# Attention products for TensorE written in its own reading order, with turned copies of v and of the weighted values

## The chip, the cores and the metric

The kernel runs on one core of one Trainium2 chip. The metric is the device time of one execution in microseconds (us); the median of three runs counts. The engines are PE (TensorE), DVE (VectorE), ACT (ScalarE), POOL (GpSimd) and SP (SyncE, which issues DMAs).

## The reference, cut to what matters

Seven convolutions turn 64 clips into 64 x 12 tokens of 192 channels; then come one attention layer and one layer of experts. The attention is a Nystrom attention: every sequence of 12 tokens is padded in front to 64, so that each of the 64 landmarks is one token, 52 of them zero.

```python
qkv = x @ w_qkv.T                       # 12 heads of 16 channels
sim = einsum('bhid,bhjd->bhij', q * scale, k)
attn1 = attn2 = attn3 = softmax(sim)    # one token per landmark
z = attn2.T / (max(col) * max(row))
for _ in range(6):
    xz = attn2 @ z
    z = 0.25 * z @ (13 * I - xz @ (15 * I - xz @ (7 * I - xz)))
out = attn1 @ (z @ (attn3 @ v))
out = out @ w_proj.T + b_proj
```

## The kernel before, in words

Attention is done lane by lane: each of the 128 partitions holds one sequence and half of the heads (HL = 6). The 52 padded tokens are folded into one, so each head has a matrix of R = 13 by 13 (`smat`), and v has SEQ = 12 rows of DH = 16. A matrix product per lane is not a thing TensorE can do, so every small product is made of two steps: all elementwise products of one output row (for example 6 heads x 13 columns x 13 terms = 1014 elements), then a sum over the terms.

The class `RowSums` (L771) describes one such job. It divides the output rows among the engines:

- `sum_pe`: DVE multiplies (L1230) into `for_pe`, and PE adds the terms: one matmul with the identity for each term (L1042), accumulating in PSUM. ACT copies the sums out (L1142). `by_term` (L790) gives the place: the buffer is laid out as (term, all columns of all rows of the batch), and the products are written into it in the order (head, column, term).
- `sum_pe_pool`: the same with POOL multiplying (L1101) into `pool_for_pe`, as a second batch in another PSUM bank.
- `by_vector`: DVE multiplies into `rowt` (L1244) and adds by a reduction (L1248).
- `by_pool`: POOL multiplies into `from_pool` (L1104) and DVE reduces (L1252).

The first factor of DVE's rows (`near`) lies in PSUM, where ACT brings it (`bring`, L1150) or where PE has left it. It is repeated over the columns.

The jobs follow each other: `scoring` (q by k, 12 rows), softmax and the norms (L1264 to L1304), `valuing` (smat by v, 13 rows, into `wv`), `outer` (smat by its transpose, into `e2`), then six iterations of `squaring` (e1 by e1) and `closing` (e2 by c4), and `applying` (e1 by wv, into `attn`). Outer, squaring and closing are made by `product` (L959). Their results are symmetric, so only the upper part is computed from row FULL = 2 on, and ACT copies the mirrored part (L1137). Between squaring and closing DVE makes c4 (L1332). A job begins when all rows of the one before are reduced and copied (the semaphores `row_done` and `copied`), in DVE's `sums` (L1227) and POOL's `multiply` (L1095). `near_ready` counts what ACT has brought: 2 before scoring, 4 before valuing, then NEAR0 = 5 and up, two each iteration.

The order of the work is written out by hand, one instruction stream for each engine; no planner is involved. No DMA is issued in the attention.

The norms: DVE takes row and column sums of smat, multiplies the padded column's sum by 1/ROOT (L1296), takes the maxima (L1298 to L1300), and combines them (L1302, L1303) for PE, which turns them (L1049). After valuing, three small DVE instructions (L1309 to L1315) give the scale.

Of the kernel before, what the change touches and what calls it, by code (L numbers as in the profile page):

```python
# [23 lines left out]
ALU = mybir.AluOpType  # L24
# [8 lines left out]
P = 128  # L33
# [43 lines left out]
SEQ = L6.pos  # L77
D, HEADS, DH = 192, 12, 16
# [692 lines left out]
class RowSums:  # L771


    def __init__(self, terms, width, sum_pe, sum_pe_pool, by_vector, by_pool, near, first, second, out, bank=0, mirror=None):
# [4 lines left out]
        self.reduced = by_vector + by_pool  # L779
        self.pooled = len(sum_pe_pool) + len(by_pool)  # L780

# [8 lines left out]
    def by_term(self, buffers, i):  # L790

        batch = next(n for n, rows in enumerate(self.batches) if i in rows)
        places, wide = self.places(self.batches[batch])
        full = buffers[batch][:, 0:self.terms * wide].rearrange("p (k n) -> p k n", k=self.terms)[:, :, places[i]]
        return full.rearrange("p k (a b) -> p a b k", a=self.first(i).shape[1])

# [62 lines left out]
def attention(nc, io, res, top):  # L859
# [35 lines left out]
    with ExitStack() as ctx:  # L895
# [13 lines left out]
        xhat = for_pe[:, 2 * TOK:2 * TOK + TT * D].rearrange("p (t c) -> p t c", t=TT)  # L909
        pool_for_pe = sb("pool_for_pe", [P, 2 * HL * R * DH])  # L910
        sum_buffers = [for_pe, pool_for_pe]
# [9 lines left out]
        padsum = sb("padsum", [P, HL])  # L921
        wv = sb("wv", [P, HL, R, DH])
        attn = sb("attn", [P, SEQ, HL * DH])
# [6 lines left out]
        def near_rows(starts, per, wide, view):  # L930
# [9 lines left out]

        scoring = RowSums(DH, lambda i: HL * SEQ, [0, 1], [6, 7], [2, 3, 4, 5], [8, 9, 10, 11],
                          lambda i: q_near(i).unsqueeze(2).broadcast_to([P, HL, SEQ, DH]),
                          lambda i: grid(q_l[:, i, :]).unsqueeze(2).broadcast_to([P, HL, SEQ, DH]),
                          lambda i: k_l.rearrange("p j (h d) -> p h j d", d=DH), lambda i: scores[:, :, i, :])
        valuing = RowSums(SEQ, lambda i: HL * DH, [0, 1, 2], [7, 8], [3, 4, 5, 6], [9, 10, 11, 12],
                          lambda i: s_near(i)[:, :, 1:R].unsqueeze(2).broadcast_to([P, HL, DH, SEQ]),
                          lambda i: smat[:, :, i, 1:R].unsqueeze(2).broadcast_to([P, HL, DH, SEQ]),
                          lambda i: v_l.rearrange("p j (h d) -> p h d j", d=DH), lambda i: wv[:, :, i, :])
        applying = RowSums(R, lambda i: HL * DH, [0, 1, 2], [6, 7], [3, 4, 5], [8, 9, 10, 11],
                           lambda i: e_near(i).unsqueeze(2).broadcast_to([P, HL, DH, R]),  # L950
                           lambda i: e1[:, :, i + 1, :].unsqueeze(2).broadcast_to([P, HL, DH, R]),
                           lambda i: wv[:, :, :, :].rearrange("p h k d -> p h d k"),
                           lambda i: grid(attn[:, i, :]))

# [3 lines left out]

        def product(a, b, out, n, near):  # L959

            def mirror(i):
                if i is None:
                    return out[:, :, 0:FULL, :], out[:, :, FULL:R, 0:FULL].rearrange("p h j i -> p h i j")
                return (out[:, :, i + 1:R, i], out[:, :, i, i + 1:R]) if i < R - 1 else None

            first = lambda i: 0 if i < FULL else i
            spread = lambda x, i: x.unsqueeze(2).broadcast_to([P, HL, R - first(i), R])
            return RowSums(R, lambda i: HL * (R - first(i)), [0, 1], [], [2, 3], [4, 5, 6, 7, 8, 9, 10, 11, 12],
                           lambda i: spread(near(i), i), lambda i: spread(a[:, :, i, :], i),
                           lambda i: b[:, :, first(i):R, :], lambda i: out[:, :, i, first(i):R], n, mirror)  # L970

        after_sums = lambda n: lambda i: sum_near[1 - n](i) if i < FULL else late_near[n](i - FULL)
        outer = product(smat, smat, e2, 0, s_near)
        squaring = product(e1, e1, e2, 0, after_sums(0))
        closing = product(e2, c4, e1, 1, after_sums(1))
        at_scoring = Before()
# [5 lines left out]

        NEAR0 = 5
        lined = lambda x: x[:, :, :, :].rearrange("p h i j -> p (h i j)")
# [18 lines left out]
        with nc.Block() as block:  # L1003
# [70 lines left out]
            def _(pool):  # L1074
# [20 lines left out]
                def multiply(job, at):  # L1095

                    if at is not at_scoring:
                        pool.wait_ge(row_done, at.reduced)
                        pool.wait_ge(copied, at.copied)
                    for i in job.sum_pe_pool:  # L1100
                        pool.tensor_tensor(job.by_term(sum_buffers, i), job.first(i), job.second(i),  # L1101
                                           ALU.mult).then_inc(pool_multiplied, 1)
                    for i in job.by_pool:
                        pool.tensor_tensor(pooled_row(job, i), job.first(i), job.second(i), ALU.mult).then_inc(pool_multiplied, 1)  # L1104
# [3 lines left out]
                multiply(scoring, at_scoring)  # L1108
                pool.wait_ge(smat_ready, 1)
                multiply(valuing, at_valuing)  # L1110
                multiply(outer, at_outer)
                pool.wait_ge(e_ready, 1)
                with pool.Fori(0, PINV_ITERS) as n:
                    multiply(squaring, at_iteration(n))
                    pool.wait_ge(cubic_ready, n + 1)
                    multiply(closing, at_iteration(n).after(squaring))
                multiply(applying, at_applying)

            @block.scalar
            def _(act):  # L1120
# [43 lines left out]
                act.wait_ge(qkv_copied[1], 2 * TT)  # L1164
                bring([bank(3, 0), bank(3, 1)], 3, 6, q_l.rearrange("p r (h k) -> p h r k", k=DH))
                copies(scoring, at_scoring)
                act.wait_ge(scores_ready, 1)
# [4 lines left out]
                bring([bank(2, 0), bank(2, 1)], 4, 7, smat)  # L1172
                copies(valuing, at_valuing)
                copies(outer, at_outer)
                act.wait_ge(e_ready, 1)
# [17 lines left out]
            def _(dve):  # L1193
# [33 lines left out]
                def sums(job, at, near, late_near=None):  # L1227
                    dve.wait_ge(near_ready, near)
                    for i in job.sum_pe:
                        ins = nc.vector.tensor_tensor(job.by_term(sum_buffers, i), job.near(i), job.second(i), ALU.mult)  # L1230
                    ins.then_inc(multiplied, 1)
# [28 lines left out]
                for half in range(2):  # L1260
# [34 lines left out]
                                                          op0=ALU.mult, op1=ALU.add))  # L1295
                steps.done(nc.vector.tensor_scalar(padsum[:, :], padsum[:, :], 1.0 / ROOT, None, ALU.mult))  # L1296
                steps.settle()
# [4 lines left out]
                nc.vector.tensor_scalar(norms[:, 0:1], norms[:, 0:1], 1.0, None, ALU.max).then_inc(peaks, 1)  # L1302
                nc.vector.tensor_scalar(norms[:, 1:2], norms[:, 1:2], scale[:, 0:1], PADS / LANDMARKS,  # L1303
                                        ALU.max, ALU.add).then_inc(peaks, 1)  # L1304

                sums(valuing, at_valuing, 4)

# [7 lines left out]
                nc.vector.tensor_scalar(top_norms[:, 2:3], top_norms[:, 1:2], -1.0, None, ALU.mult).then_inc(norm_ready, 1)  # L1315
                sums(outer, at_outer, 4)
                dve.wait_ge(scale_spread, 1)
# [10 lines left out]
                with dve.Fori(0, PINV_ITERS) as n:  # L1328
# [11 lines left out]
                nc.vector.tensor_tensor(attn[:, :, :].rearrange("p i (h d) -> p i h d", d=DH),  # L1340
                                        wv[:, :, 1:R, :].rearrange("p h i d -> p i h d"),
                                        attn[:, :, :].rearrange("p i (h d) -> p i h d", d=DH), ALU.subtract).then_inc(out_lanes, 1)
# [458 lines left out]
```

## Time and profile before

| | |
|---|---|
| runs | 998.57, 1000.88, 1007.96 us; median 1000.88 |
| the profiled execution | 1000.64 us |
| its span, first to last instruction | 998.9 us |
| PE, DVE, ACT, POOL busy | 711.4, 664.3, 301.4, 226.9 us |
| mean granted TensorE clock | 0.851 |
| convolutions | to about 560 us |
| attention | about 560 to 871.5 us |
| experts | 871.5 us to the end |

A row of a timeline has the start, the time to the last end (instructions of one kind that follow each other are merged, with their count; neighbours on an engine overlap by 0.1 or 0.2 us), engine, line, operation, names, shapes, and in brackets the idle time before and what ended it. A group has its busy time, the mean duration of one in ns, and the idle time before. In a row of stages stand the stretch, its length, then for each engine the busy time and the number of instructions, then the granted clock (1.00 is 2.4 GHz, 0.50 is 1.2 GHz), the DMA share and GB/s.

### The profile page before, as it was taken

Reading aid. Unit: us, or ns where it says so; the run is one execution under the profiler, and the core shown is the slowest. Engines: PE = TensorE matmul, PEld = TensorE weight load, DVE = VectorE, ACT = ScalarE, POOL = GpSimd, SP = SyncE. Lnnn points to the kernel's source line nnn. Section 1 sums busy time; section 2 is a strip of 40 time slices with the busy share of each in tenths; the row PEclk is TensorE's granted clock in tenths of the full one; section 3 lists DMA queues with packets and bytes.
Section 4 is the critical chain, followed back from the end, with each engine's and each line's share of the span. In section 5 each row is a group of like instructions: output and inputs, shape, how many; then the busy total and the mean of one; then the engine's idle time right before and its main releaser. Section 6 shows DMA issues by size and latency. Waiting matters only on the chain. (4 is left out here: it accounts for less than half of the span.)

```text
span 998.9 us, 10712 instructions
## 1 busy us (share of the span) xinstructions
PE 711.4 (71%) x3435; PEld 510.5 (51%) x3435; DVE 664.3 (67%) x1473; ACT 301.4 (30%) x501; POOL 226.9 (23%) x253
## 2 busy tenths in 40 slices
PE   0069997999889998999987157053444444569987
PEld 0026564656456654665554146043444444469977
DVE  4918655865577463245545557999999999656377
ACT  0043344333433353233222202002222221135433
POOL 2100000000000000000000206544666668427501
PEclk9999997999888997999985558577777676979999
DMA  1350510034000600000000600000000000010000
GB/s 54 45 116 1 106 29 1 1 45 90 1 1 11 113 0 0 1 1 1 1 1 0 265 28 1 0 0 1 0 0 0 0 0 0 9 62 1 2 1 24
DMA packets 22553, 25.29 MB, mean 25 GB/s; under 512 B 17052, under 2 KB 21212, under 8 KB 21404
## 3 DMA queue, kind: packets, MB, share of 16 engines
q1 hardware_dynamic: 22508, 24.74, 10.5%
q8 instruction: 22, 0.36, 0.2%
q14 instruction: 23, 0.19, 0.1%
HBM read 21.05 MB, written 3.66 MB: 25 GB/s over the span
## 5 line engine op out<-in xcount | busy, mean ns | idle before, releaser
L564 PE MATMUL ps<-h,w 128*128 128x400 f32 x720 | 292.6, 551 | 1.4 <-ACT h L632 1.3
L564 PEld LDWEIGHTS ps<-h,w 128*128 128x128 f32 x720 | 140.2, 201 | 106.1 <-issue 103.5
L1042 PE MATMUL pt<-for_pe,ident 128*128 128x156 f32 (+2 forms) x420 | 99.8, 420 | 108.2 <-DVE for_pe L1230 108.2
L1042 PEld LDWEIGHTS pt<-for_pe,ident 128*128 128x128 f32 x420 | 91.8, 281 | 116.1 <-DVE for_pe L1230 112.3
L724 DVE COPY h<-ps 128x800 f32<-128x800 f32 (+2 forms) x58 | 56.6, 975 | 96.2 <-PE ps L564 95.5
L577 PEld LDWEIGHTS ps<-averager,sq 128*100 128x100 f32 (+2 forms) x1024 | 101.6, 175 | 22.3 <-ACT sq L625 18.4
L577 PE MATMUL ps<-averager,sq 128*100 128x1 f32 (+2 forms) x1024 | 102.1, 230 | 7.7 <-ACT sq L625 7.3
L625 ACT ACTIVATE sq<-h 128x800 f32<-128x800 f32 (+2 forms) x58 | 49.8, 858 | 177.1 <-DVE h L724 177.1
L632 ACT ACTIVATE h<-h,lnp 128x800 f32<-128x800 f32 (+2 forms) x58 | 60.5, 1043 | 85.6 <-DVE h L755 83.8
L755 DVE TENSOR_TENSOR h<-h,ps 128x400 f32<-128x400 f32 (+2 forms) x116 | 60.0, 559 | 38.9 <-PE ps L593 38.9
L604 ACT ACTIVATE h<-ps,lnp 128x800 f32<-128x800 f32 x64 | 63.4, 1010 | 64.7 <-PE ps L525 64.5
L1075 POOL MEMSET eye<- 128x169 f32 x1 | 0.2, 241 | 346.0 <-POOLq L1742 346.0
L525 PE MATMUL ps<-late,w_stack 90*128 90x400 bf16 x128 | 36.3, 375 | 49.7 <-DMA late<-windows_dram 42.8
L1137 ACT COPY e<-e 128x60 f32<-128x60 f32 (+9 forms) x130 | 32.2, 251 | 126.0 <-DVE e L1248 102.3
L1104 POOL TENSOR_TENSOR from_pool<-e,c 128x702 f32<-128x702 f32 (+8 forms) x54 | 50.1, 968 | 34.9 <-DVE c L1332 34.9
L1252 DVE TENSOR_REDUCE e<-from_pool 128x54 f32<-128x702 f32 (+8 forms) x117 | 55.7, 559 | 0.0
L1104 POOL TENSOR_TENSOR from_pool<-e 128x702 f32<-128x702 f32 (+8 forms) x54 | 47.8, 925 | 24.2 <-ACT e L1137 16.6
L481 POOL COPY phases<-xs 128x505 f32<-128x505 f32 x4 | 7.0, 1758 | 199.8 <-DMA xs<-in_x 199.8
L525 PEld LDWEIGHTS ps<-late,w_stack 90*128 90x128 bf16 x128 | 11.5, 104 | 78.1 <-issue 61.3
L1528 PE MATMUL pf<-x_pack,w_hi 128*128 128x384 f32 x216 | 49.7, 337 | 1.4 <-ACT x_pack L1576 0.9
L671 DVE SCALAR_TENSOR_TENSOR u<-phases,gram,u 128x100 f32<-128x100 f32 x180 | 45.2, 318 | 0.9
L593 PE MATMUL ps<-rows,pick 96*128 96x400 bf16 (+2 forms) x128 | 36.6, 369 | 7.2 <-DVE rows L748 7.1
(265 smaller groups left out, 1067.2 us busy)
## 6 DMA issues: line engine op xcount, KB each, us to landing
late<-windows_dram SPq DMA_DIRECT2D x24, 375.0 KB, 7.5
gate_w<-in_gate_w SPq DMA_DIRECT2D x1, 3456.0 KB, 12.5
up_w<-in_up_w SPq DMA_DIRECT2D x1, 3456.0 KB, 19.1
windows_dram<-parts SPq DMA_DIRECT2D x12, 250.0 KB, 5.5
acts<-in_down_w SPq DMA_DIRECT2D x1, 1728.0 KB, 9.5
w<-in_w SPq DMA_DIRECT2D x1, 1024.0 KB, 6.0
xs<-in_x SPq DMA_DIRECT2D x4, 252.5 KB, 4.5
out_tokens<-hidden SPq DMA_DIRECT2D x6, 96.0 KB, 1.6
```

Source lines behind the costliest of these rows:

```text
L525: mm = pe.matmul(ypair[bank][:, h, 0:400], w0_stack[:, :], win[:, b * POS0 + h * 400:b * POS0 + h * 400 + 400], start=True, stop=True)
L564: mm = pe.matmul(out, w[:, L.first_tap + t, :], source(l, s, 2 * p + c, t), start=(t == 0), stop=(t == L.taps - 1))
L577: mm = pe.matmul(var_ps[0:L.w, at:at + 1], sq[:, n["var"] % 2, c, q * L.w:(q + 1) * L.w], averager[:, 0:1], start=True, stop=True)
L604: act.activation(h0[:, s, p, 0:POS0].rearrange("p (h t) -> p h t", h=2), ypair[b][:, :, 0:400], ACT.Gelu, scale=lnp[:, 0:1], bias=lnp[:, 1 ...
L625: act.activation(sq[:, n["conv"] % 2, :, 0:L.cols].rearrange("p c (b t) -> p c b t", t=L.pos), joined(l, s, p, r).rearrange("p (c b) t -> ...
L632: act.activation(both, both, ACT.Gelu, scale=lnp[:, 2 * l:2 * l + 1], bias=lnp[:, 2 * l + 1:2 * l + 2]).then_inc(gelu_done, 1)
L724: nc.vector.tensor_copy(joined(l, s, p, r).rearrange("p (c b) t -> p c b t", c=2), ypair[n["bank"]][:, :, 0:L.cols].rearrange("p c (b t) - ...
L755: nc.vector.tensor_tensor(h, h, spread[n["scale"] % 2][:, 0:L.cols].rearrange("p (b t) -> p b t", t=L.pos), ALU.mult).then_inc(scaled, 1)
L1042: mm = pe.matmul(pt[:, job.bank + n, 0:wide], ident[:, :], sum_buffers[n][:, k * wide:(k + 1) * wide], start=(k == 0), stop=(k == job.term ...
L1104: pool.tensor_tensor(pooled_row(job, i), job.first(i), job.second(i), ALU.mult).then_inc(pool_multiplied, 1)
L1252: nc.vector.tensor_reduce(job.out(i), pooled_row(job, i), AX.X, ALU.add).then_inc(row_done, 1)
L1528: mm = pe.matmul(out[:, n * 512:n * 512 + HALF], w, moving[:, n * HALF:(n + 1) * HALF], start=(j == 0), stop=(j == len(products) - 1))
```

## The change

1. A job may have `term_first`: then the products for PE are formed in the order (term, head, column), the order in which the buffer lies. The first factor is repeated along the innermost dimension (`by_terms`), and the second is read as (term, head, column). Scoring has none and keeps the old order.
2. In squaring and closing the second factor is read by its rows instead of its columns (`turned_rows`), which is the same by symmetry; outer, whose second factor is not symmetric, reads columns of smat.
3. `wv` is laid out (row, head, channel) instead of (head, row, channel). ACT makes two turned copies, `v_turned` after q is brought and `wv_turned` after valuing; the rows that are not for PE read those.
4. In scoring and valuing one more row goes to `sum_pe_pool` and one fewer to `by_pool`; `pool_for_pe` grows.
5. The norms: L1296 goes; its factor is in a scalar_tensor_tensor after the maxima, and one wait more stands before the last addition.
6. `near_ready` counts two more (v_turned is 3, wv_turned 6); POOL waits for 3 before valuing and for 6 before applying.

```diff
-        full = buffers[batch][:, 0:self.terms * wide].rearrange("p (k n) -> p k n", k=self.terms)[:, :, places[i]]
-        return full.rearrange("p k (a b) -> p a b k", a=self.first(i).shape[1])
+        return buffers[batch][:, 0:self.terms * wide].rearrange("p (k n) -> p k n", k=self.terms)[:, :, places[i]]
+
+    def for_pe(self, buffers, i, near):
+
+        to, heads = self.by_term(buffers, i), self.first(i).shape[1]
+        if self.term_first is None:
+            return to.rearrange("p k (a b) -> p a b k", a=heads), (self.near if near else self.first)(i), self.second(i)
+        return (to.rearrange("p k (a b) -> p k a b", a=heads), *self.term_first(i, near))
...
-        pool_for_pe = sb("pool_for_pe", [P, 2 * HL * R * DH])
+        pool_for_pe = sb("pool_for_pe", [P, 3 * HL * SEQ * DH])
...
-        wv = sb("wv", [P, HL, R, DH])
+        wv = sb("wv", [P, R, HL, DH])
+        v_turned, wv_turned = sb("v_turned", [P, HL, DH, SEQ]), sb("wv_turned", [P, HL, DH, R])
...
-        scoring = RowSums(DH, lambda i: HL * SEQ, [0, 1], [6, 7], [2, 3, 4, 5], [8, 9, 10, 11],
+        by_terms = lambda x, n: x.rearrange("p h k -> p k h").unsqueeze(3).broadcast_to([P, x.shape[2], HL, n])
+        scoring = RowSums(DH, lambda i: HL * SEQ, [0, 1], [6, 7, 8], [2, 3, 4, 5], [9, 10, 11],
...
-        valuing = RowSums(SEQ, lambda i: HL * DH, [0, 1, 2], [7, 8], [3, 4, 5, 6], [9, 10, 11, 12],
+        valuing = RowSums(SEQ, lambda i: HL * DH, [0, 1, 2], [7, 8, 9], [3, 4, 5, 6], [10, 11, 12],
...
-                          lambda i: v_l.rearrange("p j (h d) -> p h d j", d=DH), lambda i: wv[:, :, i, :])
+                          lambda i: v_turned[:, :, :, :], lambda i: wv[:, i, :, :],
+                          term_first=lambda i, near: (by_terms((s_near(i) if near else smat[:, :, i, :])[:, :, 1:R], DH),
+                                                      v_l.rearrange("p k (h d) -> p k h d", d=DH)))
...
-                           lambda i: wv[:, :, :, :].rearrange("p h k d -> p h d k"),
-                           lambda i: grid(attn[:, i, :]))
+                           lambda i: wv_turned[:, :, :, :], lambda i: grid(attn[:, i, :]),
+                           term_first=lambda i, near: (by_terms(e_near(i) if near else e1[:, :, i + 1, :], DH), wv[:, :, :, :]))
...
-                           lambda i: b[:, :, first(i):R, :], lambda i: out[:, :, i, first(i):R], n, mirror)
+                           lambda i: b[:, :, first(i):R, :], lambda i: out[:, :, i, first(i):R], n, mirror,
+                           lambda i, _: (by_terms(near(i), R - first(i)), b_turned[:, :, :, first(i):R]))
...
+        turned_rows = lambda x: x[:, :, :, :].rearrange("p h k j -> p k h j")
+        outer = product(smat, smat, smat[:, :, :, :].rearrange("p h j k -> p k h j"), e2, 0, s_near)
+        squaring = product(e1, e1, turned_rows(e1), e2, 0, after_sums(0))
+        closing = product(e2, c4, turned_rows(c4), e1, 1, after_sums(1))
...
                 bring([bank(3, 0), bank(3, 1)], 3, 6, q_l.rearrange("p r (h k) -> p h r k", k=DH))
+                act.copy(v_turned[:, :, :, :], v_l.rearrange("p j (h d) -> p h d j", d=DH)).then_inc(near_ready, 1)
                 copies(scoring, at_scoring)
...
                 copies(valuing, at_valuing)
+                act.wait_ge(row_done, at_outer.reduced)
+                act.wait_ge(copied, at_outer.copied)
+                act.copy(wv_turned[:, :, :, :], wv[:, :, :, :].rearrange("p i h d -> p h d i")).then_inc(near_ready, 1)
                 copies(outer, at_outer)
...
-                        ins = nc.vector.tensor_tensor(job.by_term(sum_buffers, i), job.near(i), job.second(i), ALU.mult)
+                        ins = nc.vector.tensor_tensor(*job.for_pe(sum_buffers, i, True), ALU.mult)
...
-                steps.done(nc.vector.tensor_scalar(padsum[:, :], padsum[:, :], 1.0 / ROOT, None, ALU.mult))
...
-                nc.vector.tensor_scalar(norms[:, 1:2], norms[:, 1:2], scale[:, 0:1], PADS / LANDMARKS,
-                                        ALU.max, ALU.add).then_inc(peaks, 1)
-
-                sums(valuing, at_valuing, 4)
+                steps.done(nc.vector.scalar_tensor_tensor(out=norms[:, 1:2], in0=scale[:, 0:1], scalar=1.0 / ROOT, in1=norms[:, 1:2],
+                                                          op0=ALU.mult, op1=ALU.max))
+                steps.settle()
+                nc.vector.tensor_scalar(norms[:, 1:2], norms[:, 1:2], PADS / LANDMARKS, None, ALU.add).then_inc(peaks, 1)
+
+                sums(valuing, at_valuing, 5)
```

## Rows read from the trace of the kernel before

**Rows 1.** Stages valuing and the iterations: PE, PEld, DVE, ACT, POOL, clock, DMA.
```profile
642.40:667.30 24.90, 12.94 (x52) 10.00 (x52) 24.83 (x16) 0.90 (x5) 12.48 (x4) 0.71 0.00 0
...
682.90:836.00 153.10, 71.04 (x312) 68.22 (x312) 147.70 (x186) 42.56 (x165) 98.28 (x109) 0.70 0.00 0
```

**Rows 2.** Timeline of all engines, one squaring, 708 to 721 us.
```profile
708.00 7.95 POOL L1104 TENSOR_TENSOR from_pool<-e 128x702 f32<-128x702 f32 x9 [3.33 <-ACT e L1137]
...
708.50 3.96 DVE L1230 TENSOR_TENSOR for_pe<-pt,e 128x1014 f32<-128x1014 f32 x2 [0.68 <-ACT e L1137]
712.28 1.94 DVE L1244 TENSOR_TENSOR rowt<-pt,e 128x858 f32<-128x858 f32 x2
...
712.51 6.14 PE L1042 MATMUL pt<-for_pe,ident 128*128 128x156 f32 x26 [6.88 <-DVE for_pe L1230]
714.11 1.91 DVE L1248 TENSOR_REDUCE e<-rowt 128x66 f32<-128x858 f32 x2
...
715.94 4.28 DVE L1252 TENSOR_REDUCE e<-from_pool 128x54 f32<-128x702 f32 x9
...
719.32 0.57 ACT L1142 COPY e<-pt 128x156 f32<-128x156 f32 x2
```

**Rows 3.** Timeline of DVE: scoring, norms, valuing and the start of outer.
```profile
612.73 2.60 DVE L1244 TENSOR_TENSOR rowt<-pt,lanes 128x1152 f32<-128x1152 f32 x2
615.24 1.34 DVE L1248 TENSOR_REDUCE scores<-rowt 128x72 f32<-128x1152 f32 x1
...
623.06 5.12 DVE L1252 TENSOR_REDUCE scores<-from_pool 128x72 f32<-128x1152 f32 x4
...
637.91 0.58 DVE L1294 SCALAR_TENSOR_TENSOR den<-smat,den 128x72 f32<-128x72 f32 x1
638.42 3.29 DVE L1296 TENSOR_SCALAR padsum<-padsum 128x6 f32<-128x6 f32 x1
...
642.41 6.22 DVE L1230 TENSOR_TENSOR for_pe<-pt,lanes 128x1152 f32<-128x1152 f32 x3
648.53 4.25 DVE L1244 TENSOR_TENSOR rowt<-pt,lanes 128x1152 f32<-128x1152 f32 x2
...
667.78 1.15 DVE L1311 TENSOR_TENSOR top_norms<-top_norms 1x1 f32<-1x1 f32 x1
```

**Rows 4.** Groups by operation and shape, DVE and POOL, attention.
```profile
L1269 DVE TENSOR_TENSOR scores<-scores,peak 128x864 f32<-128x864 f32 x1 | 1.1, 1057 | 0.0
...
L1104 POOL TENSOR_TENSOR from_pool<-smat,lanes 128x1152 f32<-128x1152 f32 x4 | 13.2, 3340 | 0.0
```

**Rows 5.** Timelines of POOL and PE in valuing, and PE's clock in the second batch.
```profile
638.37 3.32 POOL L1101 TENSOR_TENSOR pool_for_pe<-smat,lanes 128x1152 f32<-128x1152 f32 x1
...
648.68 8.03 PE L1042 MATMUL pt<-for_pe,ident 128*128 128x288 f32 x24 [5.13 <-DVE for_pe L1230]
656.55 4.06 PE L1042 MATMUL pt<-pool_for_pe,ident 128*128 128x192 f32 x24
...
656.55:660.70 4.15, 4.06 (x25) 1.00 0.00 0
```

**Rows 6.** ACT: first copies after scoring's and outer's start, and its slowest copy.
```profile
619.87 0.34 ACT L1142 COPY scores<-pt 128x72 f32<-128x72 f32 x2 [11.20 <-PE pt L1042]
...
675.91 0.30 ACT L1137 COPY e<-e 128x60 f32<-128x60 f32 x1 [14.88 <-DVE e L1248]
...
L1190 ACT COPY a_xhat_t<-pt 96x384 f32<-96x384 f32 x2 | 1.5, 852 | 7.3 <-PE pt L1063 7.3
```

**Rows 7.** Timeline of DVE in applying.
```profile
836.26 6.99 DVE L1230 TENSOR_TENSOR for_pe<-pt,wv 128x1248 f32<-128x1248 f32 x3 [0.88 <-ACT pt L1154]
842.99 4.60 DVE L1244 TENSOR_TENSOR rowt<-pt,wv 128x1248 f32<-128x1248 f32 x2
847.42 1.53 DVE L1248 TENSOR_REDUCE attn<-rowt 128x96 f32<-128x1248 f32 x1
...
859.51 1.36 DVE L1340 TENSOR_TENSOR attn<-wv,attn 128x1152 f32<-128x1152 f32 x1
```

More of the change, by code:

```diff
@@ L771, with __init__ @@
 class RowSums:
-    def __init__(self, terms, width, sum_pe, sum_pe_pool, by_vector, by_pool, near, first, second, out, bank=0, mirror=None):
+    def __init__(self, terms, width, sum_pe, sum_pe_pool, by_vector, by_pool, near, first, second, out, bank=0, mirror=None, term_first=None):
         self.batches = [rows for rows in (sum_pe, sum_pe_pool) if rows]
@@ L779, in __init__ @@
         self.reduced = by_vector + by_pool
+        self.term_first = term_first
         self.pooled = len(sum_pe_pool) + len(by_pool)
@@ L957, in attention, with product @@
         late_near = [near_rows([bank(2, n)], FULL, HL * R, mat_row) for n in range(2)]
-        def product(a, b, out, n, near):
+        def product(a, b, b_turned, out, n, near):
             def mirror(i):
@@ L969, in product @@
                            lambda i: spread(near(i), i), lambda i: spread(a[:, :, i, :], i),
-                           lambda i: b[:, :, first(i):R, :], lambda i: out[:, :, i, first(i):R], n, mirror)
+                           lambda i: b[:, :, first(i):R, :], lambda i: out[:, :, i, first(i):R], n, mirror,
+                           lambda i, _: (by_terms(near(i), R - first(i)), b_turned[:, :, :, first(i):R]))
         after_sums = lambda n: lambda i: sum_near[1 - n](i) if i < FULL else late_near[n](i - FULL)
-        outer = product(smat, smat, e2, 0, s_near)
-        squaring = product(e1, e1, e2, 0, after_sums(0))
-        closing = product(e2, c4, e1, 1, after_sums(1))
+        turned_rows = lambda x: x[:, :, :, :].rearrange("p h k j -> p k h j")
+        outer = product(smat, smat, smat[:, :, :, :].rearrange("p h j k -> p k h j"), e2, 0, s_near)
+        squaring = product(e1, e1, turned_rows(e1), e2, 0, after_sums(0))
+        closing = product(e2, c4, turned_rows(c4), e1, 1, after_sums(1))
         at_scoring = Before()
@@ L981, in attention @@
         at_applying = at_iteration(PINV_ITERS)
-        NEAR0 = 5
+        NEAR0 = 7
         lined = lambda x: x[:, :, :, :].rearrange("p h i j -> p (h i j)")
@@ L1100, in multiply @@
                     for i in job.sum_pe_pool:
-                        pool.tensor_tensor(job.by_term(sum_buffers, i), job.first(i), job.second(i),
-                                           ALU.mult).then_inc(pool_multiplied, 1)
+                        pool.tensor_tensor(*job.for_pe(sum_buffers, i, False), ALU.mult).then_inc(pool_multiplied, 1)
                     for i in job.by_pool:
@@ L1109, in _ @@
                 pool.wait_ge(smat_ready, 1)
+                pool.wait_ge(near_ready, 3)
                 multiply(valuing, at_valuing)
@@ L1116, in _ @@
                     multiply(closing, at_iteration(n).after(squaring))
+                pool.wait_ge(near_ready, 6)
                 multiply(applying, at_applying)
@@ L1315, in _ @@
                 nc.vector.tensor_scalar(top_norms[:, 2:3], top_norms[:, 1:2], -1.0, None, ALU.mult).then_inc(norm_ready, 1)
-                sums(outer, at_outer, 4)
+                sums(outer, at_outer, 5)
                 dve.wait_ge(scale_spread, 1)
@@ L1340, in _ @@
                 nc.vector.tensor_tensor(attn[:, :, :].rearrange("p i (h d) -> p i h d", d=DH),
-                                        wv[:, :, 1:R, :].rearrange("p h i d -> p i h d"),
+                                        wv[:, 1:R, :, :],
                                         attn[:, :, :].rearrange("p i (h d) -> p i h d", d=DH), ALU.subtract).then_inc(out_lanes, 1)
```

## The prediction

> **What bounds the kernel now.** I first split the span by stage. The convolutions end at about 560 us and the experts run from 871.5 us; the change touches neither, so I read only the attention between. Two of its stages stand in [rows 1]: valuing (25 us) and the six iterations of the pseudo-inverse (153 us). In both VectorE (DVE) is busy almost all the time (24.83 of 24.90 and 147.70 of 153.10), GpSimd (POOL) two thirds or less, TensorE (PE) half. So what DVE saves there the kernel saves, unless PE, ACT or POOL comes late. [Rows 2] show one product in order of time. The reader is to see three things. DVE does two rows "for PE" (L1230, 1014 elements each), then two of its own (L1244), then eleven sums. The two rows for PE take 3.78 us from start to start of what follows (708.50 to 712.28), the next two, of 858 and 780 elements, 1.83 us (to 714.11). And PE's sums begin as soon as the first two are multiplied and reach ACT at 719.32, before DVE's sums end.
>
> **Why those rows are dear, and the price of plain order.** L1230 writes its products with the term innermost, a stride of 156 floats; L1244 writes without gaps. The two plain pairs of [rows 2, 3] give a line: 1638 elements in 1.83 us, 2304 in 2.51 (612.73 to 615.24), so 1.02 ns an element and 0.08 us an instruction. I use starts, not durations, since neighbours overlap. Two rows of 1014 would take 2028 x 1.02 + 0.16 = 2.23 us instead of 3.78. A strided read costs the same as a strided write: in valuing L1244 writes plainly but reads v with a stride and takes 4.25 us for two rows, where scoring's takes 2.60 for two of the same size; and L1230, which in valuing has both strides, takes 2.04 a row (642.41 to 648.53, three rows), no more than one stride alone [rows 3]. So the price falls only where both the write and the read become plain.
>
> By "Door 1" of the Trainium skill's page "SBUF — State Buffer", an SBUF line is 16 bytes and full rate wants two hits on it: the trace agrees, 1.8 against 1.02 ns.
>
> **Part 1, the iterations.** Twelve products, each with two rows whose write becomes plain; the second factor is read in runs of 13 floats, because the iterates are symmetric. Saved: 12 x (3.78 - 2.23) = 18.6 us. The first factor now lies in PSUM and is repeated 13 times innermost. No row has such a PSUM operand. Bounds: plain price, as L1269, which repeats an SBUF operand innermost and takes 1057 ns for 864 elements [rows 4] (1.02 x 864 plus the fixed part); or the strided price, which leaves nothing (0). I take the plain one, the only row with that repetition. Nothing else is late: everything behind the two rows moves up with them. PE's start too, so its 6.8 us until ACT's copy stay 6.8. POOL's nine rows need 7.95 us from 708.00, and DVE's sums of them began 7.44 us into the product (715.94) and will begin at 5.9. POOL finishes row after row (3510 elements in all, 2.26 ns each): the first 1.1 us after DVE's start, the fifth at 5.7, the ninth at 7.5. DVE's nine sums take 4.28 us, the longest first, so it asks for the fifth at 5.9 + 4 x 0.48 = 7.8 or later. No wait. ACT's mirror copies follow DVE's sums as before.
>
> **Part 2, scoring.** Row 8 goes from DVE's sums to PE. One sum less: 5.12 / 4 = 1.28 us [rows 3]. PE's second batch grows from 144 to 216 columns; in valuing 24 matmuls of 192 took 4.06 us [rows 5], 0.88 ns a column, so 32 x 216 x 0.88 ns = 6.1 us from about 619.7 (ACT's copy of batch one at 619.87 [rows 6]), 626.3 with its copies, against DVE's end at 628.2 - 1.3 = 626.9. Just hidden. The new copy v_turned lies in ACT's idle 11.20 us [rows 6]; by ACT's dearest row, L1190 with 852 ns for 384 elements (2.2 each), it is at most 2.6 us. If it had no cover it would cost that.
>
> **Part 3, the norms.** L1296 scales six numbers and takes 3.29 us, from 638.42 until POOL's instruction of 638.37, 3.32 long, is over; L1294 (0.58 for 72 elements) ends as POOL's first one does, and L1311, one element, waits 1.15 likewise [rows 3, 5]. DVE thus waits for the end of the running POOL instruction. L1296 goes, but a scalar_tensor_tensor with two SBUF operands comes, as L1294's and L1311's are. I count it as waiting. POOL's valuing rows now read plainly: 2.26 x 1152 = 2.6 us instead of 3.34 [rows 4]. POOL's first valuing row began at 638.37 less 3.32, 635.05. All 1.28 earlier, its boundaries are 633.8, 636.4, 639.0 and 641.6. L1294, due at 636.63, now just misses one and waits to 639.0; three reductions; the new instruction waits to 641.6; valuing starts at 641.9 (before: 642.41). So of scoring's 1.28 us only 0.5 is left. If POOL's new rows stay at 3.34, both waits end earlier and valuing starts at 640.8: the other bound, 1.1 better.
>
> The Trainium skill ("SBUF — State Buffer", "Who interferes with whom") says that two SBUF inputs contend with a POOL instruction that reads SBUF, whoever is second waiting whole. This speaks against the change's new instruction. Without it valuing would start 1.9 us earlier.
>
> **Part 4, valuing.** From 641.9: three rows for PE at 1.26 (1.02 x 1152 + 0.08) instead of 2.04; four own rows whose read of v_turned is plain, like scoring's; three sums instead of four. DVE: 3.8 + 10.3 (scoring's four rows, 612.73 to 623.06) + 3.8 = 17.9, to 659.9. PE: starts at 645.9, first batch 7.87 us (648.68 to 656.55 [rows 5]), second 24 x 288 x 0.88 = 6.1, ACT's three copies 0.6: 660.5. Here PE and ACT become last, by 0.6. Against 667.3: gained so far 6.8 us.
>
> **Part 5, outer.** Its second factor is not symmetric and is read with a stride of 13: the price stays, 0 to 0.2 us gained; I take 0.1. wv_turned: at most 2.8 us of ACT's idle 14.88 there [rows 6]. Nobody waits behind it but the first mirror copy. POOL's two new waits are for copies long made.
>
> **Part 6, applying.** 1248 elements: plain 1.35 us. Three rows for PE took 6.73 (836.26 to 842.99), two own rows 4.43 (to 847.42) [rows 7]. Saved 6.73 - 4.05 = 2.7 and 3 x (2.22 - 1.35) = 2.6, together 5.3. From its start A: DVE ends at A + 23.25 - 5.3 = 18.0. POOL, from A - 0.6: six rows of 2.82, ready at A + 16.3; DVE's last sum (1.5 us, the row of 847.42) begins at 18.0 - 1.5 = 16.5. PE: A + 4.2 + 8.5 + 4.4 + 0.4 = 17.5 (valuing's batches with 13 terms for 12). Both just in time. If POOL's two rows for PE keep a strided price (3.56), DVE ends 1.1 later; that offsets the 1.1 of part 3.
>
> **Sum.** 18.6 + 6.8 + 0.1 + 5.3 = 30.8 us. The profiled execution took 1000.64 us (its span 998.9 and 1.74 around it), and the median of the runs shown is 1000.88, 0.24 more. 1000.64 - 30.8 = 969.8 for that execution, and 970.0 for the median.
>
> **Rivals.**
> - *The repeated PSUM operand keeps the strided price.* For: no row shows one. Against: L1269, and L1244's PSUM operand repeated in the middle at plain speed. Then rows for PE stay dear everywhere. Left: the start of valuing 0.5, four own rows 4 x 0.81 = 3.2, one sum 1.3, less 0.5 of PE's lateness, and applying 2.6: 7.1, so 993.7.
> - *Slower: price upon price.* The repeated operand steps from head to head out of its natural order; if that costs a second penalty of 0.76 ns an element in every row for PE: iterations 24,336 elements, +18.5 us instead of -18.6; outer +1.5; valuing's 3456 and applying's 3744 give back 2.6 and 2.8. With the 7.1 above: 7.1 - 18.5 - 1.5 - 2.6 - 2.8 = -18.3, 1019. It decides from 0.2 ns an element over today's price on. Against: two strides in one instruction cost no more than one [rows 3].
> - *PE or ACT sets the end of each product.* PE ran part of its burst at 1.2 GHz (granted clock 0.70 in the mean [rows 1]); the 0.88 ns a column were taken at granted clock 1.00 [rows 5], so a burst wholly at half of it takes 26 x 156 x 1.76 ns = 7.1 us, 0.3 over the 6.8 it has; valuing, with more columns, perhaps 2 us over. 12 x 0.3 + 2 = 5.6: 975.6. For: DVE's part shrinks, PE's doesn't. Against: both start together, and PE is not idle longer than before.
> - *It doesn't do what it says* (the new order unbuilt, or the strides still there): 1000. The diff shows the order plainly.
>
> **How the numbers follow.** Forecast 0.80, PE or ACT bound 0.14, strided PSUM price 0.035, unbuilt 0.005, slower 0.02. Range: the unknown terms are worth 1.1 down and 5.6 up, repetition between runs (998.57 to 1007.96 before) 2 or 3 either way: 966 to 977, which holds the third rival too. This kernel's measurement tells 1% from no change. Faster by over 1%: 0.94; within: 0.04; slower: 0.02.
>
> **What would show it.** L1230's successor at about 1.2 us for 1014 elements in the iterations and 1.4 in applying, yet about 2.0 in outer; product to product 1.55 us shorter; DVE still busiest; L1296 gone, the new instruction some 2 us long; POOL's valuing rows 2.6. Wrong if the successor stays near 2 us, or if DVE shows idle time in each product.

## The result and the profile after

The changed kernel took 974.47 us (median of 4 runs, 965.42 to 979.07) against 1003.65 for the kernel before (4 runs, 998.57 to 1007.96): ratio 0.970, interval 0.9612 to 0.9788. Repeated with more rounds it took 971.52 us against 1000.87, ratio 0.9698, interval 0.9658 to 0.9738. The prediction was 970.0, range 966 to 977, faster by over 1% at 0.94. The time, the sign and the size of the largest term came out; some smaller terms did not. Two stages behind applying, which the prediction held for unchanged, take different times in different executions of one kernel.

The profiled execution took 965.42 us (span 963.7), 35 less than the profiled one of before. That is more than the change gave: scoring began 4.25 us earlier (604.55 against 608.80) by work that the diff doesn't touch, and the experts took 2.4 us longer. So I compare stages, from start to start of the same DVE instructions (the second execution is the profiled one of the repetition):

| stage, us | before | predicted | after | after, second execution |
|---|---|---|---|---|
| scoring, softmax, norms | 33.61 | 33.1 | 31.80 | 31.78 |
| valuing | 24.93 | 18.6 | 18.21 | 18.81 |
| outer and first e1 | 15.61 | 15.5 | 15.49 | 15.51 |
| six iterations | 153.31 | 134.7 | 135.17 | 135.17 |
| applying | 23.25 | 18.0 | 18.02 | 18.31 |
| last subtraction to experts | 12.09 | 12.1 | 10.79 | 14.95 |
| sum | 262.80 | 232.0 | 229.48 | 234.53 |
| experts | 127.30 | 127.3 | 129.67 | 129.57 |

The experts' 2.4 us go with TensorE's granted clock: over the stage it was 0.95 before and 0.91 after, over its first 30 us 0.83 and 0.66.

```profile
871.60:998.90 127.30, 108.46 (x650) 102.36 (x650) 73.66 (x138) 53.88 (x90) 43.99 (x87) 0.95 0.06 20
...
834.03:963.70 129.67, 111.33 (x650) 105.62 (x650) 73.42 (x138) 53.98 (x90) 44.08 (x87) 0.91 0.06 19
```

The change does not decide this. Of the fourteen profiled executions of all kernels here, five have the short stage (127.3 to 127.8) and nine the long one (129.6 to 129.8), and variants of both kernels are in either group.

One squaring in the changed kernel (timeline; it answers [rows 2]):

```profile
692.08 7.96 POOL L1116 TENSOR_TENSOR from_pool<-e 128x702 f32<-128x702 f32 x9 [1.82 <-ACT e L1151]
...
692.58 2.33 DVE L1248 TENSOR_TENSOR for_pe<-pt,e 128x1014 f32<-128x1014 f32 x2 [0.68 <-ACT e L1151]
694.83 1.92 DVE L1262 TENSOR_TENSOR rowt<-pt,e 128x858 f32<-128x858 f32 x2
...
694.97 5.38 PE L1055 MATMUL pt<-for_pe,ident 128*128 128x156 f32 x26 [5.17 <-DVE for_pe L1248]
696.66 1.91 DVE L1266 TENSOR_REDUCE e<-rowt 128x66 f32<-128x858 f32 x2
...
698.49 4.28 DVE L1270 TENSOR_REDUCE e<-from_pool 128x54 f32<-128x702 f32 x9
...
701.87 0.57 ACT L1156 COPY e<-pt 128x156 f32<-128x156 f32 x2
```

The two rows for PE take 2.25 us (692.58 to 694.83) where they took 3.78, and everything behind them stands as it did: 1.83 us to the first sum, 6.9 us from PE's start to ACT's copy (6.8 before), the same 0.68 us of DVE idle in front. Nothing new is late. The groups of DVE's products say the same by place (duration in ns of one, after the comma):

```profile
L1248 DVE TENSOR_TENSOR for_pe<-pt,c 128x1014 f32<-128x1014 f32 x12 | 14.0, 1210 | 0.2
...
L1262 DVE TENSOR_TENSOR rowt<-pt,v_turned 128x1152 f32<-128x1152 f32 x4 | 5.3, 1353 | 0.1
...
L1262 DVE TENSOR_TENSOR rowt<-pt,wv_turned 128x1248 f32<-128x1248 f32 x3 | 4.3, 1451 | 0.0
L1248 DVE TENSOR_TENSOR for_pe<-pt,wv 128x1248 f32<-128x1248 f32 x3 | 4.2, 1452 | 0.9 <-ACT pt L1168 0.9
L1248 DVE TENSOR_TENSOR for_pe<-pt,smat 128x1014 f32<-128x1014 f32 x2 | 3.7, 1898 | 0.0
```

The last row is outer, where the second factor is still read with a stride: 1898 ns for the same 1014 elements that take 1210 in closing. One kernel thus holds both prices beside each other.

The norms and valuing, DVE, POOL, PE and ACT (timeline; it answers [rows 3, 5]):

```profile
629.58 6.65 POOL L1114 TENSOR_TENSOR pool_for_pe<-smat,lanes 128x1152 f32<-128x1152 f32 x3 [9.56 <-DVE smat L1302]
636.18 7.51 POOL L1116 TENSOR_TENSOR from_pool<-smat,v_turned 128x1152 f32<-128x1152 f32 x3
...
632.41 1.70 DVE L1312 SCALAR_TENSOR_TENSOR den<-smat,den 128x72 f32<-128x72 f32 x1
...
634.68 1.56 DVE L1320 SCALAR_TENSOR_TENSOR norms<-scale,norms 128x1 f32<-128x1 f32 x1
...
636.35 3.88 DVE L1248 TENSOR_TENSOR for_pe<-pt,lanes 128x1152 f32<-128x1152 f32 x3
...
640.28 7.81 PE L1055 MATMUL pt<-for_pe,ident 128*128 128x288 f32 x24 [2.79 <-DVE for_pe L1248]
647.93 5.98 PE L1055 MATMUL pt<-pool_for_pe,ident 128*128 128x288 f32 x24
...
653.95 0.52 ACT L1156 COPY wv<-pt 128x96 f32<-128x96 f32 x3 [5.30 <-PE pt L1055]
654.56 0.41 DVE L1328 TENSOR_REDUCE top_norms<-pt 1x2 f32<-1x256 f32 x1 [0.20 <-DVE wv L1270]
```

POOL's three rows for PE take 6.65 us, 2.2 each, so its instructions end near 631.8, 634.0 and 636.2 (one third of the stretch each). L1312 ends at 634.11 and the new L1320 at 636.24: both wait for POOL's running instruction, as forecast. At the end ACT's copies are last, and DVE stands 0.20 us.

### The profile page after: what moved, and what is told of

Its sections match the earlier page's. It is cut to its first block and busy times, and to the rows that moved or that the text cites. A ratio compares the mean times of both kernels' runs of the same rounds, so it can differ in the third digit from the quotient of the medians.

```text
span 963.7 us, 10716 instructions
## 1 busy us (share of the span) xinstructions
PE 711.2 (74%) x3435; PEld 511.1 (53%) x3435; DVE 631.7 (66%) x1471; ACT 306.4 (32%) x505; POOL 214.2 (22%) x253
## 5 line engine op out<-in xcount | busy, mean ns | idle before, releaser
L577 PEld LDWEIGHTS ps<-averager,sq 128*100 128x100 f32 (+2 forms) x1024 | 100.7, 173 | 22.9 <-ACT sq L625 18.6
L481 POOL COPY phases<-xs 128x505 f32<-128x505 f32 x4 | 5.0, 1258 | 199.0 <-DMA xs<-in_x 199.0
```

What stands on the lines that cost most here:

```text
L577: mm = pe.matmul(var_ps[0:L.w, at:at + 1], sq[:, n["var"] % 2, c, q * L.w:(q + 1) * L.w], averager[:, 0:1], start=True, stop=True)
```

## The experiments

Twelve runs follow, one of them of the changed kernel again and two of one and the same kernel. Stage times are from profiled executions, defined as in the table above. Where no ratio is given, the kernel ran once.

**The products alone.** Kernel before, with the new order in outer, squaring and closing only.

```diff
-            return RowSums(R, ..., lambda i: out[:, :, i, first(i):R], n, mirror)
+            return RowSums(R, ..., lambda i: out[:, :, i, first(i):R], n, mirror,
+                           lambda i, _: (by_terms(near(i), R - first(i)), b_turned[:, :, :, first(i):R]))
```

> Only outer, squaring and closing write their products for TensorE in the order term, head, column; everything else is as before. My theory (the strided write costs 0.77 us for each of 24 rows): the six iterations go from 153.3 to about 135.2 us, outer gains about 0.1, valuing and applying keep their 24.9 and 23.3 us, the whole is 18 us faster than the kernel before (ratio about 0.982). The rival (the gain needs the turned copies and the new split too, the loop is held by TensorE or ScalarE): less than 10 us.

Measured: iterations 135.16 us, outer 15.47, valuing and applying 24.93 and 23.16 as before. So 18.1 us of the gain are these 24 rows and nothing else; neither PE nor ACT held the loop. The whole kernel's ratio, 0.9817 (0.9752 to 0.9881), is some 18 us but holds anything from 12 to 25, and the medians differ by 15.6; the stage is the sharper number. In this profiled execution the stretch from the last subtraction to the experts took 15.52 us instead of 12.09 and the experts 129.60 instead of 127.30, both untouched by the diff.

**Read by columns.** Changed kernel; write plain, read strided.

```diff
-        turned_rows = lambda x: x[:, :, :, :].rearrange("p h k j -> p k h j")
+        turned_rows = lambda x: x[:, :, :, :].rearrange("p h j k -> p k h j")
```

> The changed kernel, but in squaring and closing the second factor is read by its columns (stride 13 floats, the same values by symmetry) while the write stays plain. My theory (one stride on either side costs the whole price): a row of 1014 goes back from 1.2 to about 1.9 us, the iterations from 135.2 to about 151 to 153 us, so almost the whole gain of the loop is lost although the write is plain. The rival (only the strided write costs, symmetry is not needed): the iterations stay at 135.

```profile
L1248 DVE TENSOR_TENSOR for_pe<-pt,e 128x1014 f32<-128x1014 f32 x12 | 22.5, 1922 | 3.6 <-ACT e L1151 3.2 <-ACT pt L1168 0.4
```

The iterations take 152.11 us. The plain write alone is worth 1.2 us of 18.1; without the symmetry, which lets the factor be read by its rows, the new order would be nearly useless in the iterations. Ratio 0.9857 (0.9797 to 0.9916), what valuing, applying and the norms leave.

**Both strided.** Kernel before, with the second factor of those rows in squaring and closing read with a stride too.

```diff
-                        ins = nc.vector.tensor_tensor(job.by_term(sum_buffers, i), job.near(i), job.second(i), ALU.mult)
+                        ins = nc.vector.tensor_tensor(job.by_term(sum_buffers, i), job.near(i), job.for_pe(i), ALU.mult)
...
+                           lambda i: (b[:, :, :, :] if b is smat else b[:, :, :, :].rearrange("p h k j -> p h j k"))[:, :, first(i):R, :])
```

> The kernel before, but in squaring and closing the second factor of the rows for TensorE is read with a stride of 13 floats as well (the same values by symmetry), so write and read are both strided. My theory (the two strides overlap, the dearer one counts): a row of 1014 stays at 2.0 to 2.1 us and the iterations at 153 us. The rival (price upon price): a row takes about 2.8 us and the iterations 153 + 24 x 0.76 = 171 us.

```profile
L1232 DVE TENSOR_TENSOR for_pe<-pt,e 128x1014 f32<-128x1014 f32 x12 | 23.9, 2082 | 3.6 <-ACT e L1139 3.2 <-ACT pt L1156 0.4
```

2082 ns against 2058 for the strided write alone; iterations 153.91. With the two runs above the table is full, for a row of 1014: plain and plain 1210, read strided 1922, write strided 2058, both 2082. The prices overlap. One thing differs besides: in the first two the first factor is repeated innermost, in the last two in the middle. The strides are 13 floats in the read and 156 in the write; for such a row no other strides were measured.

**Turned copies only.** Changed kernel; valuing and applying without `term_first`.

```diff
-                          lambda i: v_turned[:, :, :, :], lambda i: wv[:, i, :, :],
-                          term_first=...)
+                          lambda i: v_turned[:, :, :, :], lambda i: wv[:, i, :, :])
...
-                           lambda i: wv_turned[:, :, :, :], lambda i: grid(attn[:, i, :]),
-                           term_first=...)
+                           lambda i: wv_turned[:, :, :, :], lambda i: grid(attn[:, i, :]))
```

> The changed kernel, but valuing's and applying's rows for TensorE are written term innermost as before, now with both factors read plainly from the turned copies. My theory: each such row costs the strided write again, 2.04 instead of 1.26 us in valuing and 2.24 instead of 1.37 in applying: valuing 2.3 and applying 2.6 us longer than in the changed kernel; VectorE's own rows stay at the plain price. GpSimd's rows for TensorE go to about 2.6 us from 2.2 in valuing, since the repeated innermost operand made them cheap. The rival (the turned copies alone gave the gain): both stay within 0.5 us of the changed kernel.

Measured: valuing 21.26 us (3.05 longer; 2.3 expected), applying 20.56 (2.54 longer). The rows for PE are back at 2144 and 2397 ns, DVE's own stay at 1349 and 1455. So the turned copies serve DVE's own rows, and the new order the rows for PE. In valuing DVE's rows for PE account for 2.2 us (5.99 us for three instead of 3.79). The rest is PE: its first batch took 8.59 us instead of 7.81, at a mean granted clock of 0.70 instead of 0.77, and DVE stood 1.07 us at the end instead of 0.20.

**The old division of rows.** Changed kernel.

```diff
-        scoring = RowSums(..., [0, 1], [6, 7, 8], [2, 3, 4, 5], [9, 10, 11],
+        scoring = RowSums(..., [0, 1], [6, 7], [2, 3, 4, 5], [8, 9, 10, 11],
...
-        valuing = RowSums(..., [0, 1, 2], [7, 8, 9], [3, 4, 5, 6], [10, 11, 12],
+        valuing = RowSums(..., [0, 1, 2], [7, 8], [3, 4, 5, 6], [9, 10, 11, 12],
```

> The changed kernel with the rows divided as before (scoring 6 and 7, valuing 7 and 8 for TensorE by GpSimd, four rows in VectorE's sums each). My theory: scoring is 1.28 us longer, valuing 1.1 us longer (one sum more, less the 0.2 us by which TensorE and ScalarE are last now), from scoring's start to outer's start 2.3 us longer, up to 1 us more or less by where GpSimd's instructions end in the norms. The rival (TensorE's larger batches take the gain away): no difference or shorter.

Measured: scoring with the norms 33.27 (1.47 longer), valuing 19.29 (1.08 longer), together 2.55. The moved rows gave about what one sum each costs (1.28).

**One input in the norms.** Changed kernel.

```diff
-                steps.done(nc.vector.scalar_tensor_tensor(out=norms[:, 1:2], in0=scale[:, 0:1], scalar=1.0 / ROOT, in1=norms[:, 1:2],
-                                                          op0=ALU.mult, op1=ALU.max))
+                steps.done(nc.vector.tensor_scalar(norms[:, 1:2], norms[:, 1:2], ROOT, scale[:, 0:1], ALU.mult, ALU.max))
...
-                nc.vector.tensor_scalar(norms[:, 1:2], norms[:, 1:2], PADS / LANDMARKS, None, ALU.add).then_inc(peaks, 1)
+                nc.vector.tensor_scalar(norms[:, 1:2], norms[:, 1:2], 1.0 / ROOT, PADS / LANDMARKS, ALU.mult, ALU.add).then_inc(peaks, 1)
```

> The changed kernel with the new scalar_tensor_tensor in the norms replaced by a tensor_scalar that takes the padded sum as its per-partition scalar (one SBUF tensor input). My theory (VectorE waits for the end of GpSimd's running instruction only with two SBUF tensor inputs): it takes 0.2 instead of 1.56 us, valuing starts 1.3 to 1.4 us earlier after scoring's start. The rival (any small instruction there waits for GpSimd, as L1296 did with one input): no change.

The instruction takes 0.20 us instead of 1.56, and valuing starts 1.37 us earlier (30.43 against 31.80). But valuing then takes 19.17: PE's first batch needed 8.77 us in this execution against 7.81, DVE stood 1.17 us at the end, and most of the win was gone. The mean granted clock in the batch was 0.69 against 0.77. The earlier start is not shown to be the reason: in the four executions below in which valuing starts earlier still, 29.0 us behind scoring, the batch took 9.06, 8.09, 8.01 and 8.15 us.

**No two inputs.** The same, and L1312 and L1330 likewise: one of L1312's two operands lies in PSUM, and one of L1330's becomes the scalar.

```diff
-                steps.done(nc.vector.tensor_reduce(den[:, :, :], real, AX.X, ALU.add))
+                row_sums = pt[:, 1, 512:512 + HL * SEQ].rearrange("p (h i) -> p h i", h=HL)
+                steps.done(nc.vector.tensor_reduce(row_sums, real, AX.X, ALU.add))
...
-                steps.done(nc.vector.scalar_tensor_tensor(out=den[:, :, :], in0=smat[:, :, 1:R, 0], scalar=ROOT, in1=den[:, :, :],
+                steps.done(nc.vector.scalar_tensor_tensor(out=den[:, :, :], in0=smat[:, :, 1:R, 0], scalar=ROOT, in1=row_sums,
...
-                steps.done(nc.vector.tensor_tensor(top_norms[:, 0:1], top_norms[:, 0:1], top_norms[:, 1:2], ALU.mult))
+                steps.done(nc.vector.tensor_scalar(top_norms[:, 0:1], top_norms[:, 0:1], top_norms[:, 1:2], None, ALU.mult))
```

> As the run before, and also: the row sums of smat go to PSUM, so L1312 has one SBUF input, and the product of the two norms takes one of them as its scalar. My theory: L1312 takes 0.25 instead of 1.70 us, L1330 0.15 instead of 1.17, in all some 3.8 us less than the changed kernel from scoring's start to outer's start. The rival (the waits only move to the next instruction on VectorE): under 1.5 us.

```profile
634.66 0.28 DVE L1313 SCALAR_TENSOR_TENSOR den<-smat,pt 128x72 f32<-128x72 f32 x1
...
655.28 0.41 DVE L1328 TENSOR_REDUCE top_norms<-pt 1x2 f32<-1x256 f32 x1 [1.46 <-issue]
655.72 0.20 DVE L1330 TENSOR_SCALAR top_norms<-top_norms 1x1 f32<-1x1 f32 x1
```

With its second operand in PSUM, L1312's successor takes 0.28 us beside a running POOL instruction instead of 1.70; the product of the norms 0.20 instead of 1.17. The waits went as the theory says (2.81 us before valuing, 0.93 in outer), but the stages to the first squaring sum to 63.01 us, only 2.5 less than the 65.50 of the changed kernel, not 3.8: DVE stood 1.46 us at valuing's end for PE and ACT (the row names nobody; ACT's last copy ended 0.09 us before DVE went on). PE's first batch took 9.06 us here, at a mean granted clock of 0.67.

One row stays outside this account. L1296 of the kernel before had a single tensor input, six elements, and yet waited 3.29 us for POOL [rows 3, 5], while here instructions with one SBUF input, of one element or of 72, did not wait. Two SBUF inputs are thus not the only case, and no run isolates what L1296 met.

**Everything together.** No two inputs, and a turned copy of smat for outer, made by ACT in valuing's idle time.

```diff
+                act.copy(smat_turned[:, :, :, :], smat[:, :, :, :].rearrange("p h j k -> p k h j")).then_inc(near_ready, 1)
...
-        outer = product(smat, smat, smat[:, :, :, :].rearrange("p h j k -> p k h j"), e2, 0, s_near)
+        outer = product(smat, smat, smat_turned, e2, 0, s_near)
```

> The changed kernel, with no VectorE instruction of two SBUF inputs beside GpSimd in the norms, and with a turned copy of smat made by ScalarE during valuing so that outer's rows for TensorE are read plainly too. My theory: 3.8 us less before outer's start, and 2 x 0.72 = 1.4 us in outer: 5.2 us less than the changed kernel, ratio to the kernel before about 0.963. The rival (the freed time is taken up by TensorE's batches in valuing, which end last there): some 3 us.

The changed kernel ran again beside it:

> The changed kernel once more, with more rounds, beside the version that takes the experiments together. My theory: 29 to 33 us less than the kernel before, ratio 0.967 to 0.971, 33 us of it between scoring's start and the experts' start.

```profile
642.51 1.97 ACT L1188 COPY smat_turned<-smat 128x1014 f32<-128x1014 f32 x1
...
L1249 DVE TENSOR_TENSOR for_pe<-pt,smat_turned 128x1014 f32<-128x1014 f32 x2 | 2.3, 1192 | 0.0
```

964.06 us against 971.52, ratios to the kernel before 0.9628 (0.9578 to 0.9678) and 0.9698 (0.9658 to 0.9738). To the first squaring it needs 60.62 us, 4.9 and 5.5 less than the two executions of the changed kernel; 5.2 were expected. Outer takes 13.12 instead of 15.5. Its profiled span is 971.0 although its stages up to the experts are the shortest so far (224.57 us): scoring began at 616.88, 6 to 12 us later than in the others.

**PE kept at work, kernel before.**

```diff
                 sums(applying, at_applying)
+                for _ in range(13):
+                    pe.matmul(pt[:, 2, 0:192], ident[:, :], for_pe[:, 0:192], start=True, stop=True)
```

> The kernel before with 13 more matmuls of 192 columns into an unused bank behind applying's sums, so that TensorE is busy until shortly before it turns the heads. It tests why the changed kernel gained 1.3 us behind applying. My theory (the granted clock: TensorE stood 4.9 us before the transposes of the kernel before and 1.9 us in the changed one): the 12 transposes take 1.5 instead of 2.8 us and the heads are turned 1.3 us sooner. The rival (the gain comes from the new layout of wv or is chance): they stay at 2.8 us.

Measured: transposes 1.52 us instead of 2.79, last subtraction to experts (the tail, below) 10.81 instead of 12.09. This fitted my theory. The repetition of the changed kernel then spoiled it. Its tail, beside that of the first execution (stages: length, PE busy and instructions, granted clock, DMA share, GB/s). First execution, clock full throughout:

```profile
822.70:824.60 1.90, 0.02 (x1) 1.00 0.00 0
824.60:826.20 1.60, 1.52 (x12) 1.00 0.00 0
...
827.80:830.00 2.20, 2.17 (x13) 1.00 0.03 7
```

Second execution of the same kernel, with the same gap of 1.9 us:

```profile
826.90:828.80 1.90, 0.00 (x1) 1.00 0.00 0
828.80:831.30 2.50, 2.50 (x12) 0.57 0.00 0
831.30:832.90 1.60, 0.00 (x0) 0.50 0.00 0
832.90:835.00 2.10, 2.03 (x6) 0.50 0.00 0
```

PE worked at 2.4 GHz before the gap in both. In one it stayed there, in the other it fell to 1.2 GHz while the transposes ran, and the output projection took 7.30 us instead of 4.14. The length of the gap doesn't decide it. The other unfilled variants say so more sharply: the three long tails all stood behind a gap of 1.9 us, and four executions with longer gaps (2.3 to 2.8 us) had the short tail.

**Both gaps filled,** twice. It is the version with everything together; `fill(n)` issues n unused matmuls of 192 columns.

```diff
                 sums(applying, at_applying)
+                fill(5)
                 pe.wait_ge(out_lanes, 1)
...
                 mm.then_inc(turned, 1)
+                fill(4)
                 pe.wait_ge(to_pe, 5)
```

> The best version so far with TensorE kept at work in both gaps of the tail: 5 unused matmuls behind applying's sums (the gap of 1.9 us) and 4 behind the transposes (1.7 us). Theory (the granted clock falls only where TensorE stands): from the last subtraction to the experts 10.8 us in every execution, instead of 10.8 in some and 14.95 in others. The rival (the clock falls there by chance whatever stands in the gaps): 10.8 or about 15 as before, or more, where the unused matmuls run at half the clock.

> The same kernel in a second profiled execution, since one execution says little of a thing that differs between executions. Theory: again 10.8 us. The rival: either value.

```profile
813.68 4.39 PE L1055 MATMUL pt<-pool_for_pe,ident 128*128 128x192 f32 x26
817.90 1.79 PE L1074 MATMUL pt<-for_pe,ident 128*128 128x192 f32 x10
820.36 1.52 PE L1081 MATMUL pt<-ident,attn 128*96 128x128 f32 x12 [0.67 <-DVE attn L1366]
821.72 1.47 PE L1074 MATMUL pt<-for_pe,ident 128*128 128x192 f32 x8
823.57 4.14 PE L1088 MATMUL pt<-out_w,a_xhat_t 96*128 96x192 f32 x24 [0.39 <-ACT a_xhat_t L1215]
```

10.83 us in both. The time is 960.40 us (958.57 to 963.84), ratio 0.9572 (0.9533 to 0.9611), where the unfilled version had 964.06 (960.98 to 973.14). The two intervals overlap, and the unfilled version's profiled execution, at 972.75 one of its two slowest, had the short tail: its time was lost before scoring, which began at 616.88.

So whether filling helps is open. Of eight profiled executions of the changed kernel and its variants without filling, three had the long tail (14.95) and five the short one (10.8); two short ones in a row would come by chance in about two cases of five (5/8 squared). The two unfilled executions with the same norms as the filled kernel were short anyway. Of the kernel before and its variants, three unfilled executions took 12.09, 14.31 and 15.52 us, and the one with a filled gap 10.81.

## Why the prediction was right, and where it was not

- **Part 1, iterations: right.** 18.6 forecast, 18.1 measured. Two plain rows take 2.25 us, not 2.23, and the products alone gave all of it. The unknown, an operand in PSUM repeated innermost, has the plain price: 1210 ns. The first rival (strided price, 993.7) and the slower one (price upon price, 1019) fall with it; the run with both strides shows 2082 ns where price upon price would want about 2800.
- **Part 2, scoring: right.** DVE's sums took 3.86 us instead of 5.12; PE's wider batch took 6.00 (6.1 forecast). v_turned took 2.29 us on ACT (bound 2.6) and was hidden.
- **Part 3, norms: mechanism right, size off.** "Valuing starts at 641.9" means 0.5 us gained; it was 1.8. The term that failed is POOL's row, "2.26 x 1152 = 2.6 us": it took 2.2, so POOL's instructions ended at other places and both waits were shorter (1.70 and 1.56 where I had 2.4 and 2.0). My bounds, 2.6 and 3.34, did not hold it: I took the row's price from a factor repeated in the middle, and the innermost repetition is cheaper on POOL. The turned-copies run shows it from the other side: there POOL's rows take 2.5 us, the two waits 2.29 and 1.76, and the stage is 0.8 us longer. Without the new instruction's wait valuing started 1.37 us earlier, where I had 1.9.
- The Trainium skill's rule that I weighed there ("SBUF — State Buffer", "Who interferes with whom"), on two SBUF inputs beside a POOL instruction that reads SBUF, agrees with the trace: an instruction with two SBUF inputs waited (1.70, 1.56, 1.17 us), the same work with one of them in PSUM or as a scalar did not (0.28, 0.20, 0.20). L1296's 3.29 us, with one input, are not explained by two inputs.
- **Part 4, valuing: right within 0.4 us in the first execution.** PE and ACT were last, as forecast, by 0.2 us there instead of 0.6; in other executions they were last by more, 0.8 in the second, because PE's first batch took longer at a lower granted clock (8.41 us at 0.72 against 7.81 at 0.77). I had taken the batch's 7.87 us as fixed.
- **Part 5, outer, and part 6, applying: right.** 0.1 against 0.1; 5.23 against 5.3 (4.94 in the second execution).
- **Missed: what lies behind applying.** The prediction held it for unchanged. The tail varies with PE's clock by 4.2 us in one and the same kernel (10.79 and 14.95), so the first profile's extra 1.3 us there can't be counted as a gain of the change. The experts vary by up to 2.5 us (127.3 to 129.8 over all executions); what decides either stays open.
- **Third rival** (PE or ACT sets the end of each product, 975.6): not in the iterations, where DVE's idle time is what it was, 0.68 and 0.22 us a product; in valuing yes, by 0.2 to 1.5 us.
- **The sum.** 30.8 forecast; the stages to the experts give 33.3 in the first execution and 28.3 in the second, with the experts 30.9 and 26.0; the medians 29.2 and 29.4. The 30.9 is near for a lucky reason: the norms gave 1.3 more than forecast, valuing 0.4 and the tail 1.3 more, the iterations 0.5 less, and the experts took 2.4 more. What the diff touches, scoring to applying, was forecast at 30.8 and gave 32.0 in the first execution and 31.1 in the second.

## What to carry to other kernels

When one instruction of a family is slower than its sisters for each element, compare its innermost strides on both sides before anything else, and fit the plain price from starts of two plain sizes. A layout that made only the write plain bought 1.2 of 18 us here, and a plain read with a strided write 0.1 of 6.1 us for three rows in valuing; look for a symmetry or a copy on an idle engine that makes both plain. Beside a busy GpSimd even a one-element VectorE instruction cost 1.2 to 1.6 us when it read two tensors from SBUF; with one of them in PSUM or passed as the scalar it took 0.2 to 0.3. Compare stages, not whole executions, where what you change is smaller than what the rest varies by.

## What was not expected of the hardware

- GpSimd's product is cheaper with an operand repeated innermost: 2.2 us for 1152 elements (1.92 ns each) against 2.5 with the repetition in the middle and both factors plain (7.51 for three), and 3.34 with a strided read [rows 4].
- GpSimd's rows for PE in scoring got dearer with the wider batch: 3.03 us each for three rows (write stride 216 floats), 2.62 for two (144 floats), in the kernel before and again with the old division of rows. It held nothing up here, and the cause was not tested.
- TensorE's granted clock in the tail differed between two executions of one kernel after the same gap of 1.9 us, worth 4.2 us of 970; over 2 us in the experts went with it, and PE's first batch in valuing took 7.8 to 9.1 us in the changed kernel and its variants. A single profile can't tell such a term from a gain; several stages timed apart could.
